# Projections in one block, earlier rotation and casts, and stores of the split parts from ScalarE's queue in a four-layer transformer kernel

## The chip, the cores and the metric

The kernel runs on one core of one Trainium2 chip. The time is the device time of one execution in microseconds (us), lower is better. It is given as the median of three timed runs; one further execution was recorded by the hardware profiler, and all rows of the trace come from that one.

## The reference

The input is x, 2 batches of 1024 tokens with 128 features, float32. Four layers follow one another, each wrapped in layer norms:

```
x = x + layernorm(attention0(layernorm(x)))       # 16 heads of 64, causal
x = x + layernorm(mixture_of_experts(layernorm(x)))  # 8 experts, top 2, 128 -> 256 -> 128, exact GELU
x = x + layernorm(attention1(layernorm(x)))       # 16 heads of 8, rotary embedding
x = x + layernorm(bit_linear_ffn(layernorm(x)))   # ternary weights, relu squared
```

The change touches the seam between the second and the third layer. There it is computed, for each batch of 1024 tokens:

```
QKV = layernorm(x) @ qkv.T
q = Q * cos + rotate_half(Q) * sin                # the same for k
scores = q @ k.T / sqrt(8)                        # per head, causal; a score of exactly 0 is masked
```

## The kernel before

The five engines run programs of their own, written out by hand and tied together by semaphores. Tokens lie in four banks of 512 (NB), two for each batch. One program order per engine is fixed, so a waiting instruction holds everything behind it on its engine.

**The experts.** The mixture of experts is computed densely, one expert after the other: m = 0 to 7 for batch 0 and m = 8 to 15 for batch 1 (E is 8, so m == E + 2 is m = 10). TensorE runs, for each m, up(m + 1) and then down(m) (lines 1333 on). up(m) is four units, each a 128x512 block of hidden values into one of two banks; unit u waits until ScalarE has made the GELU of unit u - 2 (h_ready, line 1298). ScalarE makes gelus(m), four of them. down(m) fills two banks, and VectorE's sums(m) adds each of them to acc as soon as it is complete (4 operations of 128x128). down(m) waits for the sums of the expert before it.

**Attention 1's preparation for batch 0**, which rides along with batch 1's experts:

- Projections: for each of the two banks j, five products project1(j, which, bank): Q, Q with swapped halves, K, K with swapped halves, V. TensorE makes the five of j = 0 behind down(10) and the five of j = 1 behind down(11) (lines 1343 to 1351), and four PSUM banks rotate (PROJ1). ScalarE copies each out (projected1, lines 743 to 748), behind gelus(11) and gelus(12).
- Rotation: for i = 0 (Q) and i = 1 (K), VectorE multiplies the straight half by cos (rotate("cos", i), line 862), GpSimd the swapped half by sin (line 596), and VectorE adds the two (rotate("add", i), line 866). VectorE has cos 0 and cos 1 behind sums(11), add 0 and add 1 behind sums(12).
- Splitting: each float32 value becomes three bfloat16 parts. ScalarE casts the value (part(i, 0), line 639), VectorE subtracts the part (left(i, 0), line 871), ScalarE casts the rest (part(i, 1)), VectorE subtracts again and so writes the third part (left(i, 1)). ScalarE has part(0, 0) and part(1, 0) behind gelus(13), part(0, 1) and part(1, 1) behind gelus(14). VectorE has left(., 0) behind the adds and left(., 1) behind sums(13).
- Stores: SyncE writes the parts to HBM, store(0) and store(1) of 768 KB each (line 473), behind its loads of the experts' weights, the last of which waits for down(13). When both have landed (part_stored), it reads them back as stacks: stacks(half) is 18 DMAs of 64 KB, nine into QS and nine into KS, each into 8 partitions (lines 452 to 467). stacks(0) is issued first, then stacks(1).

**Attention 1** starts on TensorE when the ten copies are done, pO is cleared by VectorE behind the last sums (line 1089), and stacks(0) has landed. Batch 1's own projections, rotation and parts are made during batch 0's attention and stored by store(2) and store(3).

The numbers on a split part: split_step_of(i, j) is the count that part_a (casts) and part_v (differences) have reached when step j of part i is done.

Of the kernel before, what the change touches and what calls it, by code (L numbers as in the profile page):

```python
# [24 lines left out]
B, S, D = 2, 1024, 128  # L25
# [13 lines left out]
E, TOPK, F0 = 8, 2, 256  # L39
# [6 lines left out]
NPROB = 3  # L46
TBANKS = 3
PROJ1 = (6, 7, 2, 3)
QUEUED = 4
NMASK = 3  # L50
EPS = 1e-5
# [138 lines left out]
def build(nc, x, w0, wo0, router_w, router_b, w1, b1, w2, b2, wl1, wo1, fast_bT, w_fc, w_proj, uT, v, gate,  # L190
          consts, rotary, out):
    with ExitStack() as ctx:
# [165 lines left out]
        def split_step_of(i, j):  # L358


            return 2 * j + i + 1 if i < 2 else 2 * i + j + 1
# [4 lines left out]
        def part_of(i):  # L366
            return parts0[:, i, :, :] if i < 2 else parts1[:, :, :]

        def rotated(i, swapped):
            return rot[i // 2][:, 2 * (i % 2) + swapped, :]  # L370

# [4 lines left out]
        def _(sp):  # L376
# [92 lines left out]
            def store(i):  # L469
                sp.wait_ge(part_a, split_step_of(i, 1))  # L470
                sp.wait_ge(part_v, split_step_of(i, 1))
                b = i // 2
                sp.dma_start(split[i % 2, :, :, b * S:(b + 1) * S].rearrange("k p s -> p k s"), part_of(i)).then_inc(part_stored, 16)

            store(0)
            store(1)
            sp.wait_ge(part_stored, 32)
            stacks(0)
            stacks(1)
# [16 lines left out]
        def _(pool):  # L496
# [83 lines left out]
            for b in range(B):  # L580
                banks = range(b * NB // B, (b + 1) * NB // B)
                for j in banks:
                    power_of(2, 0, j)
                for j in banks:
                    pool.wait_ge(yn_ready[2], j + 1)
                    t = slice(j * TPB, (j + 1) * TPB)
                    pool.tensor_tensor(X[:, t, :], X[:, t, :], yn2[:, j % 2, :, :], ALU.add).then_inc(x_added[2], 1)
                for j in banks:
                    power_of(2, 1, j)
                pool.wait_ge(ld_rot, 32)  # L590
                for i in (2 * b, 2 * b + 1):
                    if b == 0:
                        pool.wait_ge(proj1_copied, 5 + 2 * i + 2)
                    else:
                        pool.wait_ge(A[1]["cp_act"], L[1].side_copied("Q", (3, 2 * (i - 2) + 1)))
                    pool.tensor_tensor(rotated(i, 1), rotated(i, 1), sin[:, :], ALU.mult).then_inc(rope_sin, 1)
# [5 lines left out]
        def _(act):  # L602
# [134 lines left out]
            for m in range(1, B * E):  # L737
                gelus(m)
                if m == E + 3:
                    for j in range(2):  # L740
                        act.wait_ge(tr_done[2], j + 1)
                        nc.scalar.copy(xnT[:, j * BANK:(j + 1) * BANK], bank[2 + j]).then_inc(xnT_ready[2], 1)
                if m in (E + 3, E + 4):
                    j = m - E - 3
                    for what in range(5):
                        u = j * 5 + what
                        act.wait_ge(proj1, u + 1)
                        projected1(j, what, bank[PROJ1[u % len(PROJ1)]]).then_inc(proj1_copied, 1)
                if m in (E + 5, E + 6):
                    part(0, m - E - 5)  # L750
                    part(1, m - E - 5)
            attention(1)


# [16 lines left out]
        def _(dve):  # L771
# [83 lines left out]
            def rotate(what, i):  # L855
                if what == "cos":
                    dve.wait_ge(ld_rot, 32)
                    if i < 2:
                        dve.wait_ge(proj1_copied, 5 + 2 * i + 1)
                    else:  # L860
                        dve.wait_ge(A[1]["cp_act"], L[1].side_copied("Q", (3, 2 * (i - 2))))
                    nc.vector.tensor_tensor(rotated(i, 0), rotated(i, 0), cos[:, :], ALU.mult).then_inc(rope_cos, 1)
                else:
                    dve.wait_ge(rope_cos, i + 1)
                    dve.wait_ge(rope_sin, i + 1)
                    nc.vector.tensor_tensor(rotated(i, 0), rotated(i, 0), rotated(i, 1), ALU.add).then_inc(rope_done, 1)
# [206 lines left out]
                    sums(E + "ym yn xm xn".split().index(what) // 2, ("ym yn xm xn".split().index(what) % 2,))  # L1073
            sums(E + 1, (1,))
            sums(E + 2, (0, 1))
            sums(E + 3, (0, 1))
            rotate("cos", 0)
            rotate("cos", 1)
            sums(E + 4, (0, 1))
            rotate("add", 0)  # L1080
            rotate("add", 1)
            left(0, 0)
            left(1, 0)
            sums(E + 5, (0, 1))
            left(0, 1)
            left(1, 1)
            sums(E + 6, (0, 1))
            sums(E + 7, (0, 1))
            nc.vector.memset(pO[:, 0:P], 0.0).then_inc(pO_cleared, 1)
# [6 lines left out]
        def _(pe):  # L1096
# [238 lines left out]
            for m in range(B * E):  # L1335
# [4 lines left out]
                    for j in range(2):  # L1340
                        transpose1(j, bank[2 + j]).then_inc(tr_done[2], 1)
                down(m)
                if m in (E + 2, E + 3):
                    j = m - E - 2
                    pe.wait_ge(xnT_ready[2], 2)
                    pe.wait_ge(added, NT + E * ST)
                    for which in range(5):
                        u = j * 5 + which
                        if u >= len(PROJ1):
                            pe.wait_ge(proj1_copied, u - len(PROJ1) + 1)  # L1350
                        project1(j, which, bank[PROJ1[u % len(PROJ1)]]).then_inc(proj1, 1)
# [70 lines left out]
```

## Time and profile before

| | us |
|---|---|
| timed runs | 1264.19, 1263.3, 1258.38 |
| median | 1263.3 |
| profiled execution | 1254.74 |
| its span, first to last instruction | 1252.9 |
| TensorE matmul busy | 1112.5 |
| VectorE busy | 862.9 |
| ScalarE busy | 814.4 |
| GpSimd busy | 349.4 |

The span is what the trace covers; the 1.8 us beside it lie before the first and behind the last instruction. The experts of batch 1 run from about 677 to 753 us of the span, attention 1 from 769 us on. In the views PE is TensorE, DVE VectorE, ACT ScalarE, POOL GpSimd, SP SyncE, and SPq what SyncE's queue issues. L and a number is a line of the kernel. A time in a timeline is the start in us from the span's start, followed by the duration; a group of several instructions stands as one row with its count, and the brackets at the end hold the idle time of the engine ahead of it and what ended it.

### The profile page before, as it was taken

The page shows a single profiled execution, that of the slowest core. Times are in us where ns is not written, and L with a number is a line of the kernel's source. Part 1 is how long each engine was busy: PE and PEld are TensorE (multiplying, and loading weights), DVE is VectorE, ACT ScalarE, POOL GpSimd, SP SyncE. Part 2 cuts the span into 40 slices and gives each one's busy share as a digit, 9 for nine tenths or more (in the row PEclk, how much of TensorE's full clock was granted, in tenths as well). Part 3 has the DMA queues.
Part 4 walks back from the last instruction along what each step waited for, and adds up shares of the span by engine and source line. Part 5 has one row for each costly group of instructions (what it writes and reads, how often), then busy time and mean ns, then how long its engine had stood idle before and what let it go on. Part 6 is the DMA issues. An engine that isn't in the chain of part 4 may idle for free.

```text
span 1252.9 us, 28180 instructions
## 1 busy us (share of the span) xinstructions
PE 1112.5 (89%) x10202; PEld 844.8 (67%) x10202; DVE 862.9 (69%) x2486; ACT 814.4 (65%) x1915; POOL 349.4 (28%) x345
## 2 busy tenths in 40 slices
PE   3799999999999999999799983897788888888886
PEld 1587878787888878789566661565556556556674
DVE  4565656565656565655433554999999999999954
ACT  2566666666666676750234441898989989989923
POOL 1596464545455555504000111010000000000033
PEclk9899999999999999999699995898999999999999
DMA  3222232222223232200101115020302212110001
GB/s 109 70 57 68 59 85 59 71 73 69 75 68 75 68 76 69 68 19 26 39 26 43 30 69 74 3 39 27 64 8 33 27 14 40 18 24 2 2 1 34
DMA packets 33147, 58.90 MB, mean 47 GB/s; under 512 B 4810, under 2 KB 18018, under 8 KB 33010
## 3 DMA queue, kind: packets, MB, share of 16 engines
q1 hardware_dynamic: 33010, 57.10, 20.0%
q8 instruction: 83, 1.36, 0.5%
q14 instruction: 54, 0.44, 0.1%
HBM read 27.59 MB, written 4.33 MB: 25 GB/s over the span
## 4 chain that ended last, share of the span: by engine, by line
PE 56%; DVE 18%; issue 11%; ACT 7%; POOL 5%; DMA 3%; SPq 1%; ACTq 0%; POOLq 0%; DVEq 0%
PE pT L1237 12%; PE pO L1160 12%; PE pS L1198 10%; DVE Zb L914 9%; PE pS L1299 4%; PE pT L1108 4%; PE pT L1312 3%; ACT probs L688 3%; DVE Sm L929 3%; PE pS L1260 2%; PE pT L1112 2%; ACT PT L668 1%; PE pS L1379 1%; PE pS L1359 1%; DMA KS<-split 1%
## 5 line engine op out<-in xcount | busy, mean ns | idle before, releaser
L1237 PE MATMUL pT<-cst,probs 128*128 128x128 f32 x2304 | 367.1, 285 | 55.2 <-ACT probs L688 50.9
L1237 PEld LDWEIGHTS pT<-cst,probs 128*128 128x128 f32 x2304 | 255.2, 142 | 149.5 <-ACT probs L688 100.3
L688 ACT ACTIVATE probs<-probs,nmax 128x128 f32<-128x128 f32 (+7 forms) x256 | 198.6, 776 | 131.9 <-DVE nmax L924 130.9
L668 ACT COPY PT<-pT 128x512 f32<-128x512 f32 (+3 forms) x576 | 263.1, 480 | 15.0 <-PE pT L1237 13.9
L924 DVE CUSTOM_DVE_ANT_0 probs<-pS,causal_wide 128x128 f32<-128x128 f32 (+7 forms) x256 | 192.0, 750 | 92.9 <-PE pS L1198 85.2
L688 ACT ACTIVATE probs<-Sm,nmax 128x128 f32<-128x128 f32 (+7 forms) x256 | 199.4, 779 | 61.2 <-DVE nmax L929 55.4
L1160 PE MATMUL pO<-PT,V 128*64 128x128 f32 (+1 forms) x4608 | 231.4, 279 | 1.9 <-DVE attnT L883 1.1
L914 DVE TENSOR_SCALAR Zb<-pS 128x128 bf16<-128x128 f32 (+7 forms) x256 | 192.7, 753 | 21.5 <-PE pS L1204 21.2
L1160 PEld LDWEIGHTS pO<-PT,V 128*64 128x64 f32 (+1 forms) x4608 | 180.6, 114 | 34.4 <-issue 19.9
L929 DVE CUSTOM_DVE_ANT_0 Sm<-pS,Zb 128x128 f32<-128x128 f32 (+7 forms) x256 | 193.3, 755 | 4.5
L512 POOL TENSOR_TENSOR rstd<-rstd,power 128x4 f32<-128x4 f32 x32 | 32.6, 1017 | 553.3 <-DVE rstd L782 553.2
L966 DVE COPY PT<-pT 128x256 f32<-128x256 f32 (+3 forms) x192 | 99.8, 520 | 115.9 <-PE pT L1237 114.6
L1198 PE MATMUL pS<-Kh,Qs 128*128 128x512 f32 (+2 forms) x384 | 159.0, 423 | 7.2 <-DMA Kl<-Kl 7.2
L1198 PE MATMUL pS<-KS,QS 72*128 72x512 bf16 (+3 forms) x384 | 108.4, 337 | 25.8 <-DMA KS<-split 15.9
L1198 PE MATMUL pS<-Kl,Qs 128*128 128x512 f32 (+2 forms) x384 | 128.8, 344 | 0.0
L1198 PEld LDWEIGHTS pS<-Kh,Qs 128*128 128x128 f32 x384 | 73.3, 191 | 27.8 <-issue 21.6
L1198 PEld LDWEIGHTS pS<-Kl,Qs 128*128 128x128 f32 x384 | 73.5, 191 | 20.3 <-issue 14.6
L729 ACT ACTIVATE hT<-pS,b1s 128x512 f32<-128x512 f32 x64 | 43.7, 687 | 57.2 <-PE pS L1299 57.2
L555 POOL TENSOR_TENSOR Ql<-raw,Qs 64x512 fp32r<-64x512 f32 x60 | 76.5, 1276 | 4.8
L555 POOL TENSOR_TENSOR Kl<-raw,Kh 64x512 fp32r<-64x512 f32 x60 | 76.5, 1275 | 4.8
L1064 DVE SCALAR_TENSOR_TENSOR acc<-pT,router,acc 128x128 f32<-128x128 f32 x112 | 31.5, 344 | 66.1 <-PE pT L1312 66.1
L575 POOL TENSOR_TENSOR attnT<-attnT,wq_t 128x1024 f32<-128x1024 f32 x16 | 38.3, 2391 | 118.9 <-DMA wq_t<-factors 118.4
(183 smaller groups left out, 1361.5 us busy)
## 6 DMA issues: line engine op xcount, KB each, us to landing
Qs<-Ql SPq DMA_DIRECT2D x32, 256.0 KB, 3.7
Kh<-Kh SPq DMA_DIRECT2D x32, 256.0 KB, 3.4
Kl<-Kl SPq DMA_DIRECT2D x32, 256.0 KB, 4.6
wq_t<-factors SPq DMA_DIRECT2D x32, 256.0 KB, 4.0
QS<-split SPq DMA_DIRECT2D x72, 64.0 KB
KS<-split SPq DMA_DIRECT2D x72, 64.0 KB
split<-parts SPq DMA_DIRECT2D x4, 768.0 KB, 4.0
w1s<-in_w SPq DMA_DIRECT2D x16, 128.0 KB, 2.2
```

The costliest lines, as they stand in the source:

```text
L555: i = pool.tensor_tensor(low[h], source[rows[h], :], high[h].bitcast(F32), ALU.subtract)
L668: nc.scalar.copy(PT[:, g % 2, h, k0 * P:(k0 + nk) * P], pT[r % TBANKS][:, 0:nk * P])\
L688: nc.scalar.activation(probs[:, i % NPROB, 0:n], src[:, 0:n], ACT.Exp, bias=nmax[:, i % 4:i % 4 + 1], scale=-1.0, accum_out=total).then_in ...
L914: nc.vector.tensor_scalar(Zb[:, i % NMASK, 0:n], pS[i % 2][:, 0:n], 0.0, MASKED, ALU.is_equal, ALU.mult).then_inc(a["z"], 1)
L924: nc.vector.tensor_tensor_reduce(probs[:, i % NPROB, 0:n], pS[i % 2][:, shift(k, qt):shift(k, qt) + n], causal_wide[:, S - n:S], -1.0, 3e3 ...
L929: nc.vector.tensor_tensor_reduce(Sm[:, i % NMASK, 0:n], pS[i % 2][:, 0:n], Zb[:, i % NMASK, 0:n], -(DH1 ** -0.5), 3e38, ALU.add, ALU.min, ...
L966: nc.vector.tensor_copy(PT[:, gg % 2, hh, k0 * P:(k0 + nk) * P], pT[r % TBANKS][:, 0:nk * P])\
L1108: return nc.tensor.matmul(p, w0s[:, what, :], xnT[:, b * S + j * BANK:b * S + (j + 1) * BANK], start=True, stop=True)
L1160: m = nc.tensor.matmul(pO[rows, 0:P], v, PT[:, g % 2, h, kt * P:(kt + 1) * P], start=(kt == 0), stop=(kt == qt), skip_group_check=True)
L1198: m = nc.tensor.matmul(pS[i % 2][:, (off + c0) * P:(off + c1) * P], lhs, keys[:, b if k == 0 else half % 2, h, c0 * P:c1 * P], start=(n == 0),
L1237: m = nc.tensor.transpose(pT[r % TBANKS][:, kt * P:(kt + 1) * P], probs[:, item % NPROB, (k0 + kt) * P:(k0 + kt + 1) * P], ident)
L1299: nc.tensor.matmul(bank[u % 4 if m < E else u % 2], w1s[:, m % 2, f * P:(f + 1) * P], xnT[:, j * BANK:(j + 1) * BANK], start=True, stop=Tr ...
```

## The change

Six edits, in the order of the data:

1. TensorE makes all ten projections behind down(10). Their order is now by kind, both banks of each kind after one another (PROJECTIONS), so that Q is complete with the second, its swapped form with the fourth, K with the sixth and its swapped form with the eighth.
2. ScalarE copies all ten behind gelus(11).
3. The waits for proj1_copied follow: 4i + 2 for cos (before 5 + 2i + 1), 4i + 4 for sin (before 5 + 2i + 2).
4. VectorE has cos 0, cos 1 and add 0 ahead of sums(11), add 1 and left(., 0) behind it, left(., 1) behind sums(12), and sums(13) after that.
5. ScalarE has part(., 0) behind gelus(12) and part(., 1) behind gelus(13).
6. store(0) and store(1) are issued by ScalarE behind gelus(14), after it has waited for both kinds of split step. SyncE only waits for part_stored. store(2) and store(3) stay on SyncE.

```diff
+PROJECTIONS = [(j, which) for which in (0, 1, 2, 3, 4) for j in range(2)]
...
+        def split_of(i):
+            return split[i % 2, :, :, i // 2 * S:(i // 2 + 1) * S].rearrange("k p s -> p k s")
...
             def store(i):
                 sp.wait_ge(part_a, split_step_of(i, 1))
                 sp.wait_ge(part_v, split_step_of(i, 1))
-                b = i // 2
-                sp.dma_start(split[i % 2, :, :, b * S:(b + 1) * S].rearrange("k p s -> p k s"), part_of(i)).then_inc(part_stored, 16)
-
-            store(0)
-            store(1)
+                sp.dma_start(split_of(i), part_of(i)).then_inc(part_stored, 16)
+
             sp.wait_ge(part_stored, 32)
             stacks(0)
...
                     if b == 0:
-                        pool.wait_ge(proj1_copied, 5 + 2 * i + 2)
+                        pool.wait_ge(proj1_copied, 4 * i + 4)
...
-                if m in (E + 3, E + 4):
-                    j = m - E - 3
-                    for what in range(5):
-                        u = j * 5 + what
+                if m == E + 3:
+                    for u, (j, what) in enumerate(PROJECTIONS):
                         act.wait_ge(proj1, u + 1)
                         projected1(j, what, bank[PROJ1[u % len(PROJ1)]]).then_inc(proj1_copied, 1)
-                if m in (E + 5, E + 6):
-                    part(0, m - E - 5)
-                    part(1, m - E - 5)
+                if m in (E + 4, E + 5):
+                    part(0, m - E - 4)
+                    part(1, m - E - 4)
+                if m == E + 6:
+                    for i in range(2):
+                        act.wait_ge(part_a, split_step_of(i, 1))
+                        act.wait_ge(part_v, split_step_of(i, 1))
+                        nc.scalar.dma_start(split_of(i), part_of(i)).then_inc(part_stored, 16)
...
                     if i < 2:
-                        dve.wait_ge(proj1_copied, 5 + 2 * i + 1)
+                        dve.wait_ge(proj1_copied, 4 * i + 2)
...
             sums(E + 2, (0, 1))
-            sums(E + 3, (0, 1))
             rotate("cos", 0)
             rotate("cos", 1)
-            sums(E + 4, (0, 1))
             rotate("add", 0)
+            sums(E + 3, (0, 1))
             rotate("add", 1)
             left(0, 0)
             left(1, 0)
-            sums(E + 5, (0, 1))
+            sums(E + 4, (0, 1))
             left(0, 1)
             left(1, 1)
+            sums(E + 5, (0, 1))
             sums(E + 6, (0, 1))
...
-                if m in (E + 2, E + 3):
-                    j = m - E - 2
+                if m == E + 2:
                     pe.wait_ge(xnT_ready[2], 2)
                     pe.wait_ge(added, NT + E * ST)
-                    for which in range(5):
-                        u = j * 5 + which
+                    for u, (j, which) in enumerate(PROJECTIONS):
```

## Rows read from the trace of the kernel before

**Rows 1.** The page's first section: busy us of each engine, share of the span, instructions.
```profile
PE 1112.5 (89%) x10202; PEld 844.8 (67%) x10202; DVE 862.9 (69%) x2486; ACT 814.4 (65%) x1915; POOL 349.4 (28%) x345
```

**Rows 2.** Waits, 670 to 770 us: who waited for whom, us, times, longest.
```profile
PE pS L1198 <- DMA KS<-split: 15.9, 1, 15.9
```

**Rows 3.** The chain that ended last, 730 to 880 us: start, us, what.
```profile
746.06 4.43 DMA split<-parts
756.35 12.78 DMA KS<-split
```

**Rows 4.** Timeline of TensorE, 675 to 770 us: start, duration, operation, count.
```profile
706.95 1.02 PE L1124 MATMUL pT<-xnT,wl1s 128*128 128x512 f32 x2
...
711.27 3.79 PE L1299 MATMUL pS<-xnT,w1s 128*128 128x512 f32 x8
714.90 3.73 PE L1312 MATMUL pT<-w2s,hT 128*128 128x128 f32 x32
...
722.79 3.79 PE L1299 MATMUL pS<-xnT,w1s 128*128 128x512 f32 x8
...
735.30 3.65 PE L1299 MATMUL pS<-xnT,w1s 128*128 128x512 f32 x4 [3.43 <-ACT hT L729]
738.74 3.81 PE L1312 MATMUL pT<-w2s,hT 128*128 128x128 f32 x32
...
746.01 7.31 PE L1312 MATMUL pT<-w2s,hT 128*128 128x128 f32 x64
769.26 0.27 PE L1198 MATMUL pS<-KS,QS 72*128 72x128 bf16 x1 [15.94 <-DMA KS<-split]
```

**Rows 5.** Timeline of VectorE, 675 to 770 us.
```profile
716.88 1.13 DVE L1064 SCALAR_TENSOR_TENSOR acc<-pT,router,acc 128x128 f32<-128x128 f32 x4 [8.61 <-PE pT L1312]
...
720.22 1.22 DVE L862 TENSOR_TENSOR rot<-rot,cos 128x1024 f32<-128x1024 f32 x1 [0.42 <-ACT rot L630]
721.93 2.80 DVE L862 TENSOR_TENSOR rot<-rot,cos 128x1024 f32<-128x1024 f32 x1 [0.49 <-ACT rot L630]
...
743.64 2.35 DVE L871 TENSOR_TENSOR parts<-rot,parts 128x1024 bf16<-128x1024 f32 x2
...
754.51 0.17 DVE L1089 MEMSET pO<- 128x128 f32 x1
```

**Rows 6.** Timeline of SyncE's queue, 670 to 770 us: issues.
```profile
742.59 0.38 SPq L450 DMA_DIRECT2D w2s<-in_w  x1
744.93 1.50 SPq L473 DMA_DIRECT2D split<-parts  x2
750.50 0.30 SPq L464 DMA_DIRECT2D QS<-split  x1
...
756.35 0.30 SPq L466 DMA_DIRECT2D KS<-split  x1
```

**Rows 7.** Windows: stretch, us, engines' busy us (x instructions), PEclk (1.00 is full), DMA share, GB/s.
```profile
735.30:737.00 1.70, 1.70 (x2) 0.71 (x3) 0.62 (x1) 0.53 (x1) 0.00 (x0) 0.55 0.00 0
745.00:750.00 5.00, 5.00 (x39) 4.47 (x39) 2.32 (x6) 2.66 (x3) 0.00 (x0) 1.00 0.84 314
753.00:769.00 16.00, 0.32 (x3) 0.13 (x2) 1.29 (x5) 0.00 (x0) 0.00 (x0) 0.59 0.55 72
```

**Rows 8.** Timeline of ScalarE, 675 to 770 us.
```profile
708.01 0.58 ACT L630 COPY rot<-pT 128x512 f32<-128x512 f32 x1 [3.66 <-PE pT L1124]
708.87 0.58 ACT L630 COPY rot<-pO 128x512 f32<-128x512 f32 x1 [0.27 <-PE pO L1124]
...
726.62 0.69 ACT L729 ACTIVATE hT<-pS,b1s 128x512 f32<-128x512 f32 x1 [0.17 <-PE pS L1299]
```

**Rows 9.** Timeline of GpSimd, 675 to 770 us.
```profile
721.11 5.82 POOL L596 TENSOR_TENSOR rot<-rot,sin 128x1024 f32<-128x1024 f32 x2 [21.98 <-ACT rot L630]
```

**Rows 10.** The parts' tile: the stores (count, min/median/max ns of an issue) and their landing.
```profile
L473 SPq DMA_DIRECT2D split<-parts x4: 366/380/382, 744.9 to 885.0; - x4
...
DMA to landing us min/median/max: 3.5/4.0/5.3
```

## The prediction

> **What bounds the kernel now.** I read the page first: TensorE has by far the largest busy share, 89% [rows 1], so a gain must shorten a stretch in which it runs or waits. The waits of the stretch from batch 1's experts to the second attention come next. Two waits of TensorE stand out there: 15.9 us of the first score matmul for the stacked K parts (KS) [rows 2], and 3.43 us of an expert's first-layer matmul (L1299) for a GELU [rows 4]. The chain in order of time says what the large one is made of: the stores of the split parts (4.43 us to landing), then 18 stack loads, of which the last takes 12.78 us to land [rows 3]. The timelines give the dates. TensorE ends the last expert at 746.01 + 7.31 = 753.32 and starts attention at 769.26 [rows 4]. VectorE clears pO by 754.51 + 0.17 = 754.68 [rows 5]. SyncE issues the stores at 744.93, goes on at 750.50 with the stacks and issues the last one of stacks(0) at 756.35 [rows 6]. So attention starts when the parts have gone out and come back, 14.6 us after everything else is ready. Whatever moves the landing of stacks(0) moves attention, and what follows it, until that slack is gone.
>
> How long is the round trip? From the first store's issue to the first stack's: 750.50 - 744.93 = 5.57 us. From there to attention: 769.26 - 750.50 = 18.76 us. The stacks are limited by the transfer: in 753 to 769 us the queues move 72 GB/s at a DMA share of 0.55, while the stores moved 314 GB/s [rows 7]. An earlier start doesn't change either speed, so I take both durations over unchanged.
>
> **1. The projections in one block.** Five take 711.27 - 706.95 = 4.32 us of TensorE [rows 4]; the other five move ahead of up(12) and down(11) and cost the same 4.32. The copies on ScalarE follow one every 0.86 us (708.01, 708.87) and take 0.58 [rows 8]; four banks rotate, and the copy four back is long done, so TensorE doesn't wait. Ten projections last 706.95 to 715.59, then up(12) 3.63, down(11) 3.57: up(13) starts at 722.79 as before. On TensorE this part alone is worth nothing. What it buys is the dates of the copies: the second (Q complete) ends at 708.87 + 0.58 = 709.45 instead of 720.11, the fourth at 711.2, the sixth at 712.9, the eighth at 714.6.
>
> **2. Rotation earlier.** VectorE is free between sums(10), over by the time of the first copy, and down(11)'s first half. That half comes 1.98 us after down's start in today's rows (716.88 against 714.90) [rows 4, 5], so at 719.22 + 1.98 = 721.2. In between go cos 0 (1.22 us, from 709.6) and cos 1 (from 713.0), and GpSimd's two sine products (5.82 us for both now [rows 9]) from 711.3 to at most 719. cos 1 takes 2.80 us today beside GpSimd, against 1.22 alone [rows 5]; priced at 2.80 it ends at 715.8, and "add 0" at 2.8 more ends by 718.6. All of it fits ahead of 721.2, so it costs nothing; if it didn't, sums(11) would slip by the rest, and TensorE needs those sums only at down(12), 7 us later. Then sums(11) ends near 724.0 and "add 1" (half of 2.35) at 725.2.
>
> **3. Casts earlier.** ScalarE ends gelu(12) at 715.59 + 4.52 = 720.1 (4.52 is from up's start 722.79 to gelu's end 726.62 + 0.69 [rows 4, 8]). It casts part(0,0), then waits for "add 1" until 725.2 and casts until 726.25. Behind this wait stand the GELUs of expert 13, and behind them TensorE: up(13) can do two of its four units (722.79 to 724.67) and then waits for gelu(13) unit 0, some 0.65 us long. It goes on at 726.9, a wait of 2.3 us. So the 3.4 us wait isn't removed; it moves one expert ahead and shrinks by 1.1 to 1.2 us.
>
> **4. The clock behind that wait.** Today the last two units after the wait (735.30 to 738.74) take 3.44 us instead of 1.81, and the granted clock there is 0.55 of full, that is the lower level of 1.2 GHz [rows 4, 7]; the loss is 1.63 us. Before it TensorE stood still for 3.43 us. After a wait of 2.3 us the clock may hold or fall: 0 or 1.63 us. I take 0, since the wait is a third shorter and TensorE is busy throughout before it, and keep 1.63 for the range.
>
> **5. To the end of gelu(14).** The rest of up(13) ends at 726.9 + 1.81 = 728.7, down(12) at 732.3, gelu(14) at 732.3 + 4.52 = 736.8. Meanwhile ScalarE makes the second casts after gelu(13) (729.5 to 731.6, ahead of the first unit of up(14) at 733.4, so hidden), and VectorE does sums(12) until 733.6 and then the two last differences (2.35 us [rows 5]) until 736.0, 0.8 us ahead of 736.8. Should they be late, ScalarE waits in front of gelu(15), whose first unit arrives only at 739.5 + 1.06 = 740.5 (1.06 from the start of a product of this shape, 706.95, to its reader, 708.01 [rows 4, 8]): 3.7 us of cover.
>
> **6. Stores from ScalarE's queue.** On SyncE they would stand behind the load of w2s for expert 15, which waits for down(13): 742.59 today [rows 6], 739.5 then. From ScalarE they go at 736.9. No row shows a DMA issued by ScalarE. On SyncE an issue holds the queue 0.38 us; even ten times that would be covered by the 3.7 us ahead of gelu(15). The landing I bound by rows: 5.57 us from first issue now, of which the second store, issued last, needs 4.43 [rows 3, 6]. With both issued together it lies between 4.43 + 0.38 = 4.8 and, by the longest landing of a store (5.3) behind the 1.50 that the two issues take today, 6.8 [rows 6, 10]. I take 5.57, as both are held up by 1.57 MB going through. Landed: 742.5. The Trainium skill speaks against this part ("DMA: Bandwidth & Descriptors", "Issuing engines are not separate DMA queues"): starting DMAs on several engines only saves the sequencer's issue time. By that alone the two issues, 0.76 us, would be all; [rows 6] show a wait for down(13) ahead of them in the same queue, and that, 2.6 us, is what I count.
>
> **7. The stacks.** SyncE waits there by 739.9 and issues stacks(0) at 742.5; they land at 742.5 + 18.76 = 761.3. Next latest are TensorE at 753.32 - 2.8 = 750.5 and the clearing of pO at 751.9, so the stacks still decide, with some 10 us to spare. The sum: 769.26 - 761.3 = 8.0 us. Attention then starts after an idle of over 10 us, as today after 15.9 us, and the clock has every reason to be where it is today (0.59 over 753 to 769 [rows 7]), so nothing is added or lost behind it; batch 1's own parts stay with SyncE.
>
> **The sum and the time.** The profiled execution lasted 1254.74 us, its span 1252.9; minus 8.0 that is 1246.7. The median of the three timed runs is 1263.3, 8.6 above the profiled one, and I forecast against it: 1263.3 - 8.0 = 1255.3 us.
>
> **The rivals.**
> (a) The clock falls behind the new wait too. All from up(13) to gelu(14) then moves 1.63 us back, since ScalarE can issue the stores only behind gelu(14): gain 6.4 us, 1256.9. For it: the same shape of wait dropped it today. Against it: 2.3 us is shorter. Chance 0.2.
> (b) ScalarE's queue is dearer than SyncE's, or casts and sums slip past gelu(14): 2 to 5 us of the gain go. The margin of VectorE in step 5 is only 0.8 us. Near 1259. Chance 0.17.
> (c) The order doesn't bring what it says: the wait for "add 1" grows (sine products and sums in one another's way), TensorE stands as long as now, and the stores get away little earlier than now. About 1262. Chance 0.08.
> (d) Slower: the stores from ScalarE run at the stacks' speed instead of the stores' own. 1.57 MB at 72 GB/s [rows 7] is 21.8 us instead of 5.6; they would land at 736.9 + 21.8 = 758.7 and attention would start at 777.5, 8.2 us later than now: 1271.5. It decides from a landing of 5.6 + 8.0 = 13.6 us. The four stores of today, of the same shape, all landed within 3.5 to 5.3 us [rows 10], which speaks against it. Chance 0.05.
>
> **How the numbers follow.** The likeliest case, steps 1 to 7 with gains of 7 to 9 us, has 0.5. The range takes in (a), (b) and most of (c), and the spread of the runs shown (1258.38 to 1264.19): 1247.5 to 1263. Half a percent is 6.3 us, about what a measurement of this kernel can tell from no change. The likeliest case lies 1.7 us past it, (a) at its edge, (b) and (c) within: faster 0.57, within 0.37, slower 0.06.
>
> **What would show it.** In the changed profile: ten L1124/L1126 projections in a row from about 707 to 715.6; TensorE's wait for hT near 724.7 of about 2.3 us, with a granted clock of 1.0 behind it (0.55 is (a)); stores issued on ScalarE's queue near 737, some 8 us ahead of today's; the first stack 5.6 us behind them; attention near 761.3, with a wait of TensorE for KS of 10.8 us instead of 15.9; the distance from there to the end as now, some 484 us. The prediction is wrong if the first stack comes more than 7 us after the stores' issue, if gelu(14) ends after 738.5, or if the stacks take clearly more or less than 18.8 us.

## The result and the profile after

| | before | after |
|---|---|---|
| median of 12 timed runs, us | 1263.59 | 1252.61 |
| lowest to highest, us | 1258.29 to 1266.76 | 1249.19 to 1257.91 |
| span of the profiled execution, us | 1252.9 | 1250.1 |

The ratio of after to before is 0.9932, with a 95% interval of 0.9913 to 0.9951. Two later batches gave 0.9962 (0.9943 to 0.9981) and 0.9938 (0.9915 to 0.9961) for the same kernel. So the change makes the kernel faster, by 0.4 to 0.7%, that is 5 to 9 us, with 7 us as the mean of the three ratios. The forecast was 8.0 us. The two medians of a batch lie 11.0, 7.0 and 8.1 us apart. In the first batch the runs of the kernel before fall into two groups, four at 1258.3 to 1259.1 and eight at 1263.3 to 1266.8, and a median taken from such groups jumps, so the text goes by the ratios.

The two spans differ by only 2.8 us. That is the first thing to explain, because the prediction was worked out on the profiled execution.

TensorE in the changed kernel (timeline: start, duration, operation, count, idle time ahead of it and what ended it), to be held against [rows 4]:

```profile
707.04 1.02 PE L1128 MATMUL pT<-xnT,wl1s 128*128 128x512 f32 x2
...
715.69 3.79 PE L1303 MATMUL pS<-xnT,w1s 128*128 128x512 f32 x8
...
722.89 1.88 PE L1303 MATMUL pS<-xnT,w1s 128*128 128x512 f32 x4
727.07 1.98 PE L1303 MATMUL pS<-xnT,w1s 128*128 128x512 f32 x4 [2.30 <-ACT hT L730]
728.89 3.73 PE L1316 MATMUL pT<-w2s,hT 128*128 128x128 f32 x32
...
743.27 7.31 PE L1316 MATMUL pT<-w2s,hT 128*128 128x128 f32 x64
764.00 0.27 PE L1202 MATMUL pS<-KS,QS 72*128 72x128 bf16 x1 [13.42 <-DMA KS<-split]
```

The ten projections fill 707.04 to 715.69. The wait for a GELU is there, one expert earlier, and lasts 2.30 us instead of 3.43. Attention starts at 764.00 instead of 769.26.

VectorE, for [rows 5], and GpSimd, for [rows 9]:

```profile
713.08 1.76 DVE L866 TENSOR_TENSOR rot<-rot,cos 128x1024 f32<-128x1024 f32 x1 [2.21 <-ACT rot L631]
714.76 1.21 DVE L870 TENSOR_TENSOR rot<-rot 128x1024 f32<-128x1024 f32 x1
...
724.13 1.22 DVE L870 TENSOR_TENSOR rot<-rot 128x1024 f32<-128x1024 f32 x1
...
733.70 2.35 DVE L875 TENSOR_TENSOR parts<-rot,parts 128x1024 bf16<-128x1024 f32 x2
```

```profile
711.40 2.35 POOL L597 TENSOR_TENSOR rot<-rot,sin 128x1024 f32<-128x1024 f32 x1 [12.18 <-ACT rot L631]
714.77 3.41 POOL L597 TENSOR_TENSOR rot<-rot,sin 128x1024 f32<-128x1024 f32 x1 [1.02 <-ACT rot L631]
```

The second add starts only at 724.13, behind sums(11), though its two inputs were ready at 718.2. ScalarE, for [rows 8], with the stores that are now in its stream (ACTq):

```profile
720.10 1.03 ACT L640 CAST parts<-rot 128x1024 bf16<-128x1024 f32 x1
725.38 1.04 ACT L640 CAST parts<-rot 128x1024 bf16<-128x1024 f32 x1 [4.24 <-DVE rot L870]
...
736.28 0.69 ACT L730 ACTIVATE hT<-pS,b1s 128x512 f32<-128x512 f32 x1 [0.17 <-PE pS L1303]
736.34 2.51 ACTq L755 DMA_DIRECT2D split<-parts  x2
740.71 0.69 ACT L730 ACTIVATE hT<-pS,b1s 128x512 f32<-128x512 f32 x1 [3.74 <-PE pS L1303]
```

SyncE's queue, for [rows 6]:

```profile
739.85 0.38 SPq L454 DMA_DIRECT2D w2s<-in_w  x1
743.00 0.30 SPq L468 DMA_DIRECT2D QS<-split  x1
```

And two windows, for [rows 7]: behind the wait the clock is at its upper level (1.00, 2.4 GHz); the stacks' transfer moves 63 GB/s where the kernel before had 72.

```profile
727.07:728.90 1.83, 1.83 (x5) 0.87 (x6) 0.61 (x1) 1.19 (x2) 0.00 (x0) 1.00 0.00 0
743.00:764.00 21.00, 7.58 (x66) 7.18 (x65) 4.67 (x17) 2.27 (x3) 0.00 (x0) 0.73 0.52 63
```

Where the 8 us went in this pair of executions can be added up. The first stack is 7.5 us earlier (743.00 against 750.50). The transfer of stacks(0) takes 21.0 us instead of 18.76, which gives 2.24 back. Attention to the third layer's output projection takes 423.2 us (764.00 to 1187.16) instead of 422.3 (769.26 to 1191.59), which costs 0.83. The rest takes 62.9 us instead of 61.3, which costs 1.63 more, and this last part is one row: the last product of the kernel ran 5.47 us in the changed kernel and 3.84 us in the one before. First the row of the kernel before, then that of the changed one:

```profile
1240.84 3.84 PE L1379 MATMUL pS<-wq_t,relu 128*128 128x128 f32 x32 [1.92 <-ACT relu L767]
```

```profile
1236.41 5.47 PE L1381 MATMUL pS<-wq_t,relu 128*128 128x128 f32 x32 [1.92 <-ACT relu L771]
```

7.5 - 2.24 - 0.83 - 1.63 = 2.8 us. The question for the experiments is which of these belong to the change and which to the execution.

### The profile page after: what moved, and what is told of

The parts are those of the page before. It is cut to its first block, busy times and chain, and to the rows that moved or that the text cites. A ratio compares the mean times of both kernels' runs of the same rounds, so it can differ in the third digit from the quotient of the medians.

```text
span 1250.1 us, 28179 instructions
## 1 busy us (share of the span) xinstructions
PE 1113.9 (89%) x10202; PEld 846.4 (68%) x10202; DVE 862.7 (69%) x2486; ACT 814.1 (65%) x1915; POOL 349.3 (28%) x345
## 4 chain that ended last, share of the span: by engine, by line
PE 55%; DVE 18%; issue 11%; ACT 6%; POOL 5%; DMA 3%; SPq 1%; ACTq 0%; POOLq 0%; DVEq 0%
PE pT L1241 12%; PE pO L1164 12%; PE pS L1202 10%; DVE Zb L918 9%; PE pS L1303 4%; PE pT L1112 4%; DVE Sm L933 3%; PE pT L1316 3%; ACT probs L689 3%; PE pS L1264 2%; PE pT L1116 2%; PE pS L1381 1%; DMA KS<-split 1%; PE pS L1361 1%; ACT PT L669 1%
```

## The experiments

Theory: attention starts when stacks(0) has landed; the change moves the first stack by some 7.5 to 8 us and nothing else. Rivals: the change also slows the stacks, as they now start while the experts still run; an issue on another queue is worth only its own time; the wait for a GELU isn't on the path; something other than the stacks' landing sets the start.

To compare executions, all dates in the table are counted from the first projection (the first L1124 or L1128 row of TensorE's timeline), since that date itself moves from execution to execution (last column). First store and first stack are the issues of these DMAs, attention is the first score product, and transfer is the time from the first stack's issue to it. Each row is one profiled execution.

| kernel | first store | first stack | experts end | attention | transfer | first projection |
|---|---|---|---|---|---|---|
| before | 37.98 | 43.6 | 46.4 | 62.3 | 18.8 | 706.95 |
| again_before | 37.95 | 43.5 | 46.3 | 64.3 | 20.8 | 711.67 |
| block_only | 37.97 | 43.5 | 46.4 | 64.5 | 21.0 | 711.14 |
| after | 29.30 | 36.0 | 43.5 | 57.0 | 21.0 | 707.04 |
| again_after | 29.30 | 36.0 | 43.5 | 57.1 | 21.1 | 705.83 |
| again_after2 | 29.30 | 35.2 | 43.5 | 54.0 | 18.7 | 706.75 |
| stores_sync | 33.3 | 39.0 | 43.6 | 59.9 | 20.9 | 707.01 |
| add_first | 26.9 | 32.8 | 41.2 | 54.0 | 21.2 | 711.60 |
| store_twice | 35.5 (second pair) | 41.1 | 46.4 | 61.9 | 20.8 | 705.62 |
| stacks1_late | 29.30 | 36.0 | 43.5 | 55.0 | 19.0 | 711.09 |
| order_fast | 24.2 | 31.6 | 41.2 | 52.5 | 21.0 | 708.69 |
| fast_late | 24.2 | 31.6 | 41.2 | 52.0 | 20.4 | 711.86 |
| keys_gpsimd | 29.30 | 35.7 | 43.5 | 54.4 | 18.7 | 711.64 |
| fast_late_gpsimd | 24.2 | 31.2 | 41.2 | 47.1 | 15.9 | 708.13 |

The time in us behind each name below is the median of its 4 to 12 timed runs; the ratio is to the kernel before in the same batch, with its 95% interval.

**The two kernels again.** No edit.

> The kernel before once more, unaltered, for its profile. Its profiled execution lasted 1254.74 us, below each of its 59 timed ones, and its stacks(0) took 18.76 us to land, while seven others with the same loads took 20.8 to 21.2. If that 18.76 was a favourable execution, this one shows about 21.0 us from the first stack to attention and 1257 to 1265 us in all; if the kernel before has the shorter transfer as its own (its stacks begin when the experts are nearly over), it shows 18.8 again. Counted from its first projection, the stores are issued at 37.98 and the first stack at 43.56 in either case.

> The changed kernel once more, unaltered. In its profile the dates up to the first stack load came out as forecast (stores issued at 736.3, first stack at 743.0), but stacks(0) took 21.0 us to land instead of the 18.76 us of before, and from the start of attention to the end it took 486.1 us instead of 483.6. If both are chance of the one execution, this profile shows again 743.0 for the first stack (within 0.3), a transfer that may as well be 18.8 us, and another distance to the end. If the change slows the stacks (their first loads now run beside the last experts), the transfer is 21 us again. Timed: 0.993 of before, by the theory that the date of the first stack moves everything by some 7.5 us.

> The changed kernel a third time, on the chip of the three others of this batch. Dates counted from the first projection: stores at 29.3, first stack at 36.0, attention at 57.0 (transfer 21). Time between 0.993 and 0.996 of before, between the two ratios measured so far.

Measured: again_before 1261.5 us, again_after 1256.2 us with 0.9962, again_after2 1253.4 us with 0.9938. The profile of again_before, TensorE and the window of the transfer:

```profile
711.67 1.02 PE L1124 MATMUL pT<-xnT,wl1s 128*128 128x512 f32 x2
...
775.93 0.26 PE L1198 MATMUL pS<-KS,QS 72*128 72x128 bf16 x1 [17.92 <-DMA KS<-split]
```

```profile
755.18:775.90 20.72, 2.82 (x26) 2.64 (x25) 2.83 (x11) 0.00 (x0) 0.00 (x0) 0.66 0.52 64
```

The same of again_after2:

```profile
706.75 1.02 PE L1128 MATMUL pT<-xnT,wl1s 128*128 128x512 f32 x2
...
760.70 0.27 PE L1202 MATMUL pS<-KS,QS 72*128 72x128 bf16 x1 [10.40 <-DMA KS<-split]
```

```profile
742.00:760.70 18.70, 8.29 (x67) 7.63 (x67) 4.67 (x17) 2.66 (x3) 0.00 (x0) 0.78 0.52 72
```

Both kernels show both transfers: 18.7 or 18.8 us at 72 GB/s and about 21 us at 63 to 64 GB/s. The change isn't what slows the stacks: again_before has the slower transfer without it and again_after2 the faster one with it. The profiled execution of before was one with the faster transfer. Like with like, the gain at the start of attention is 64.3 - 57.0 = 7.3 us with the slower transfer and 62.3 - 54.0 = 8.3 us with the faster one. Of the 1.0 us between these two, 0.7 lies in the landing of the stores, as the first stack of again_after2 comes at 35.2 instead of 36.0. The slower transfer doesn't use fewer DMA engines: the share is 0.52 in both, and the packets moved are nearly as many (814 in before, 804 in the changed kernel), so a packet takes some 14% longer. Why stays open.

The last column explains a part of the rest of the scatter. Up to the first projection the programs are the same, and still that date lies between 705.6 and 711.9. The windows of 600 to 640 us, where the router ends and the first experts start, show why. Before, then again_before, and below each of them its row of the same 24 products:

```profile
600.00:640.00 40.00, 34.45 (x153) 24.04 (x153) 14.42 (x90) 12.61 (x19) 0.00 (x0) 0.76 0.12 37
622.66 3.01 PE L1331 MATMUL pT<-b2s,wgT 8*128 8x128 f32 x24
```

```profile
600.00:640.00 40.00, 35.49 (x136) 25.16 (x135) 13.30 (x86) 9.86 (x15) 0.00 (x0) 0.60 0.09 30
623.26 5.48 PE L1331 MATMUL pT<-b2s,wgT 8*128 8x128 f32 x24
```

A granted clock of 0.76 against 0.60 (a mean of its two levels), and 153 against 136 products done. The first projection comes 4.7 us later, of which 0.6 is there ahead of these 24 products: more than half of what the change is worth, between two executions of one kernel. All fourteen profiles go this way: the six with the first projection at 711.1 to 711.9 have a granted clock of 0.60 or 0.61 in this stretch, the eight at 705.6 to 708.7 have 0.72 to 0.79.

Two more parts scatter behind the start of attention. From there to the kernel's last product it takes 471.6 to 476.1 us, which no experiment here explains, and that product itself takes 3.84 us in two profiles (before, fast_late) and 5.46 or 5.47 in the other twelve, the one of again_before among them. So the profile that the prediction was worked out on had the faster transfer, the shortest attention and the faster last product.

**block_only**: the first part alone.

```diff
-                if m in (E + 2, E + 3):
-                    j = m - E - 2
+                if m == E + 2:
...
-                    for which in range(5):
-                        u = j * 5 + which
+                    for u, (j, which) in enumerate(PROJECTIONS):
...
-                        pool.wait_ge(proj1_copied, 5 + 2 * i + 2)
+                        pool.wait_ge(proj1_copied, 4 * i + 4)
...
-                        dve.wait_ge(proj1_copied, 5 + 2 * i + 1)
+                        dve.wait_ge(proj1_copied, 4 * i + 2)
```

(ScalarE's copies likewise.)

> The kernel before with the first part of the change alone: ten projections in one block, ScalarE's ten copies behind gelus(11), the waits for the copies renumbered; rotation, casts and stores stay where they are. Theory: the block alone is worth nothing, because the casts still come behind sums(12) and gelus(13). TensorE's wait for a GELU shrinks only if the adds do come earlier, which they can't, as they stand behind sums(12). VectorE's cos 1 no longer meets GpSimd, but nobody waits for it. First stack at 750.5, attention near 769.3, time as before, within 0.2%. Rival (the earlier copies pay by themselves): part of the 8 us shows.

Measured: 1260.2 us, ratio 0.9984 (0.9958 to 1.001).

```profile
711.14 1.02 PE L1123 MATMUL pT<-xnT,wl1s 128*128 128x512 f32 x2
...
739.51 3.02 PE L1298 MATMUL pS<-xnT,w1s 128*128 128x512 f32 x4 [3.44 <-ACT hT L730]
```

From the first projection on, every date is that of before within 0.1 us, the 3.44 us wait included. The block is worth nothing by itself on the path. The median is 2.9 us below that of before in its batch and its interval takes in 1, so it doesn't contradict that.

**stores_sync**: part 6 undone.

```diff
-                if m == E + 6:
-                    for i in range(2):
-                        act.wait_ge(part_a, split_step_of(i, 1))
-                        act.wait_ge(part_v, split_step_of(i, 1))
-                        nc.scalar.dma_start(split_of(i), part_of(i)).then_inc(part_stored, 16)
...
+            store(0)
+            store(1)
             sp.wait_ge(part_stored, 32)
```

> The changed kernel with the two stores back on SyncE's queue, behind the load of w2s for expert 15. Theory (head of the line): the stores are issued at 740.3, when that load has been issued (739.85 + 0.4), instead of 736.3 on ScalarE; the first stack follows 5.6 us later, at 745.9 instead of 743.0, and attention starts 2.9 us later than in the changed kernel; time 1255.5. Rival (an issue on another queue only saves the time of issuing): start within 0.8 us of the changed kernel's, time unchanged at 1252.6.

Measured: 1259.2 us, ratio 0.9979 (0.9959 to 1.0); again_after in the same batch had 0.9962.

```profile
739.82 0.38 SPq L454 DMA_DIRECT2D w2s<-in_w  x1
740.30 0.94 SPq L476 DMA_DIRECT2D split<-parts  x2
745.99 0.30 SPq L468 DMA_DIRECT2D QS<-split  x1
```

The stores stand right behind the load that waits for down(13), as expected to the tenth, 4.0 us later than in the changed kernel; they land in 5.7 us instead of 6.7, and so attention is 3.0 us later (59.92 against 56.96). The medians differ by 3.0 us too, though the two intervals overlap, so the dates carry this reading. (The 1255.5 us expected had been counted from 1252.6 for the changed kernel, and that had 1256.2 in this batch.) ScalarE's queue saves a place in line. The rest of the gain, 64.3 or 64.5 (again_before, block_only) to 59.9, is 4.3 to 4.6 us and belongs to the earlier rotation and casts, which need the block. The Trainium skill ("DMA: Bandwidth & Descriptors", "Issuing engines are not separate DMA queues") counts only the sequencer's issue time; the trace shows 0.94 us for both issues, and attention 3.0 us earlier, because the queue passed by was waiting.

**add_first**: the second add ahead of sums(11).

```diff
             rotate("add", 0)
-            sums(E + 3, (0, 1))
             rotate("add", 1)
+            sums(E + 3, (0, 1))
```

> The changed kernel with VectorE's second add ahead of sums(11) instead of behind it. Both sine products are over at 718.2, the sums come at 721.3, so the add (1.2 us) fits. ScalarE's second cast then follows the first at once (721.1 to 722.2), gelus(13) isn't held up, and TensorE's wait of 2.30 us disappears. Theory (the chain of forecast steps 3 to 7): everything behind up(13) comes 2.3 us earlier, stores at 734.0, first stack at 740.7, attention 2.3 us earlier than in the changed kernel; time 1250.3. Rival (the wait isn't on the path, as attention waits for the stacks and TensorE has slack): TensorE's experts end 2.3 us earlier, but attention starts at the same time.

Measured: 1250.7 us, ratio 0.9916 (0.9887 to 0.9944), 5.4 us under again_after in its batch. TensorE has no wait for a GELU any more; up(13) runs through in one piece, and the stores follow:

```profile
727.45 3.79 PE L1303 MATMUL pS<-xnT,w1s 128*128 128x512 f32 x8
```

```profile
738.53 1.50 ACTq L755 DMA_DIRECT2D split<-parts  x2
```

Counted from the first projection, the stores come at 26.9 instead of 29.3, which is the 2.3 us of the wait, and attention at 54.0 instead of 57.0 with the same slower transfer. So the wait was on the path, by way of gelus(14) and not by way of the experts. The other 0.7 us is the landing of the stores, 5.9 us instead of 6.7, below. The 5.4 us between the medians is more than the 3.0 us that the dates show; the two intervals leave room for that.

**store_twice**: the outward trip doubled (the declarations of spare and spared are left out).

```diff
+                        nc.scalar.dma_start(spare[i, :, :, 0:S].rearrange("k p s -> p k s"), part_of(i)).then_inc(spared, 16)
+                    act.wait_ge(spared, 32)
+                    for i in range(2):
                         nc.scalar.dma_start(split_of(i), part_of(i)).then_inc(part_stored, 16)
```

> The changed kernel in which ScalarE first stores both parts (1.57 MB) to a spare place in HBM, waits until they have landed and then stores them again to their own place. It doubles the outward half of the round trip. Theory: the first stack comes some 6.5 us later (from 743.0 to 749.5), and attention with it, from near 763 to 769.5; gelus(15) are held up by the wait too, up to 742.9, some 2 us, which has no price since TensorE's experts still end by 753.5. Time 1259 to 1260. Rival (attention is set by something else, such as the experts): well under 6 us.

Measured: 1260.0 us, ratio 0.9994 (0.9975 to 1.0013).

```profile
734.92 2.02 ACTq L757 DMA_DIRECT2D spare<-parts  x2
741.15 0.91 ACTq L760 DMA_DIRECT2D split<-parts  x2
742.10 1.26 ACT L732 ACTIVATE hT<-pS,b1s 128x512 f32<-128x512 f32 x2 [6.56 <-DMA spare<-parts]
```

The first stack comes 5.1 us later than in the changed kernel, not 6.5, since the second pair landed 5.6 us after its issue, and attention comes 5.0 us later, with a transfer of 20.8 us. Of the 7.3 us that the change gains with the slower transfer 2.4 are left (64.3 against 61.9); the ratio of 0.9994 is back near 1, and its interval leaves room for such a rest. The experts end at 46.4, 15.6 us ahead of attention, so they don't set its start; the landing of the parts does.

**stacks1_late** and **fast_late**: stacks(1) only after four score tiles.

```diff
             stacks(0)
+            sp.wait_ge(A[1]["s"], 4)
             stacks(1)
```

> The changed kernel in which SyncE issues stacks(1) only after the first four score tiles, so that stacks(0) has the queues for itself. Theory (the loads of one queue go one after the other on each DMA engine, and the engines that a stack uses are full from stacks(0) alone): its transfer takes 18.8 to 21 us as before, at most 1 us less. Rival (stacks(1) takes a share): by the 0.15 MB that it moved in that time next to the 1.18 MB of stacks(0), 2 to 2.5 us less, with attention earlier by as much.

> The faster order (second add ahead of sums(11), differences between the halves of the sums, stores between the GELUs of expert 14) and stacks(1) issued only after four score tiles. Counted from the first projection the first stack comes at 31.6, as in the faster order alone. Theory (stacks(1) takes a share of the DMA engines, 0.14 MB of 1.32 in the transfer): the transfer is 19.0 us instead of 21.0, as it was with stacks(1) held back in the changed kernel, attention at 50.5 instead of 52.5, time 0.988 of before. Rival (the 18.97 us was a favourable execution like the one of before): 21 us, time 0.989.

Measured: stacks1_late 1253.6 us, 0.9933 (0.9904 to 0.9962), transfer 19.0 us; fast_late, on top of order_fast below, 1251.0 us, 0.9917 (0.9899 to 0.9936), transfer 20.4 us. The first seemed to bear out that stacks(1) takes a share. The second, by its own expectation, speaks for the rival: 20.4 us instead of the 19.0 hoped for, and no gain over order_fast. Between these two, holding stacks(1) back saves 0.6 us of the 21. The 19.0 us is near the 18.7 that the kernels unaltered in this respect show too, though here 1.18 MB was moved in it instead of some 1.35; what part of it was the hold can't be told from one profile.

**order_fast**: everything as early as the experts' order allows (store(i) has the two waits and the issue; the block behind gelus(14) goes).

```diff
             rotate("add", 0)
-            sums(E + 3, (0, 1))
             rotate("add", 1)
+            sums(E + 3, (0,))
             left(0, 0)
+            sums(E + 3, (1,))
             left(1, 0)
-            sums(E + 4, (0, 1))
+            sums(E + 4, (0,))
             left(0, 1)
             left(1, 1)
+            sums(E + 4, (1,))
...
+                    if m == E + 6 and u in (1, 3):
+                        store(u // 2)
```

> The changed kernel, built so that the parts are finished as early as this order of the experts allows: second add ahead of sums(11), each difference between the two halves of sums(11) and sums(12), and the stores issued by ScalarE between the GELUs of expert 14 (the first ahead of unit 1, the second ahead of unit 3). Expected dates: no wait of TensorE at up(13), last difference done near 732, stores at 731.5 and 734, landed near 738, first stack 5 us earlier than in the changed kernel (738 against 743.0), attention 5 us earlier. Stores of 1.25 us each hold up the GELUs of expert 14, and TensorE with them by 1 to 2 us, without a price, as TensorE has 13 us of slack. Time 1247.5. Rival (holding up the GELUs costs the clock or the path): above 1250.

Measured: 1249.7 us, ratio 0.9891 (0.9869 to 0.9913).

```profile
732.79 0.69 ACT L737 ACTIVATE hT<-pS,b1s 128x512 f32<-128x512 f32 x1 [1.87 <-PE pS L1307]
732.85 0.38 ACTq L728 DMA_DIRECT2D split<-parts  x1
733.65 0.69 ACT L737 ACTIVATE hT<-pS,b1s 128x512 f32<-128x512 f32 x1 [0.17 <-PE pS L1307]
734.69 0.69 ACT L737 ACTIVATE hT<-pS,b1s 128x512 f32<-128x512 f32 x1 [0.36 <-PE pS L1307]
734.75 0.37 ACTq L728 DMA_DIRECT2D split<-parts  x1
```

Attention comes 4.4 us earlier than in the changed kernel, with the same transfer of 21.0 us. The GELUs are not held up at all, where over 1 us for each store was expected: each issue takes 0.37 us and runs beside the GELU ahead of it.

**keys_gpsimd** and **fast_late_gpsimd**: the nine K loads of stacks(0) from GpSimd's queue; the second on top of fast_late.

```diff
+                if b == 0:
+                    pool.wait_ge(part_stored, 32)
+                    for row in range(0, STACK, DH1):
+                        j = row // DH1 % PARTS
+                        pool.dma_start(KS[row:row + DH1, 0, :, :],
+                                       split[1, j:j + 1, 0:HPG * DH1, 0:S].rearrange("k (h d) s -> k d h s", h=HPG)
+                                       .rearrange("k d h s -> (k d) h s")).then_inc(ld_keys, 16)
```

(SyncE leaves them out, and TensorE waits for ld_keys too.)

> The changed kernel in which the nine K loads of stacks(0) are issued by GpSimd, while SyncE issues the nine Q loads and then stacks(1). In the trace the loads of 8 partitions use the DMA queues at a share of 0.55 and 63 to 72 GB/s, whereas the stores of 128 partitions went at 314. Theory (the stacks' own transfer, 18.8 to 21 us, is the largest term, and it is slow because each load runs on half of the DMA engines): if GpSimd's loads go to other engines too, the transfer falls to 12 to 15 us, attention starts 5 to 8 us earlier than in the changed kernel, time 1245 to 1248. The Trainium skill ("DMA: Bandwidth & Descriptors", "Why a DMA increments its semaphore by 16 and not by 1") says that GpSimd's loads take their engines in turn and SyncE's always the lowest-numbered ones. Rival (all loads go to the same engines): nothing, or a loss by GpSimd's slower issue.

> The same, and the nine K loads of stacks(0) issued by GpSimd. With stacks(1) behind SyncE's nine Q loads, GpSimd's loads landed 5.9 us after their issue (median) and the last one 13.6 us, while the DMA share rose from 0.55 to 0.87 for a while. Theory (GpSimd's loads use the DMA engines that SyncE's leave idle, and only those that meet SyncE's are slow): with stacks(1) held back SyncE's queue is empty after some 0.59 MB, 9 to 10 us, so the transfer falls to 10 to 13 us and attention starts at 42 to 45, close behind the end of the experts at 41.2. Time 0.982 to 0.985 of before, 1241 to 1245. Rival (something else makes the loads slow, such as the distance to HBM): 17 to 19 us, no faster than the version without GpSimd.

Measured: keys_gpsimd 1253.9 us, 0.9919 (0.9898 to 0.9941), transfer 18.7 us; fast_late_gpsimd 1242.7 us, **0.9851 (0.9832 to 0.9871)**, transfer 15.9 us. In keys_gpsimd the transfer was no shorter than the faster level of the other kernels, a miss: the last K load landed 13.6 us after its issue, beside the loads of stacks(1). With stacks(1) held back the last one takes 10.8 us. The windows of fast_late_gpsimd, and the landing of GpSimd's loads:

```profile
739.36:744.50 5.14, 5.14 (x30) 3.35 (x29) 0.86 (x4) 4.03 (x5) 4.86 (x9) 1.00 0.72 128
744.50:750.00 5.50, 4.80 (x43) 4.61 (x42) 3.52 (x14) 0.00 (x0) 0.23 (x1) 1.00 0.67 73
750.00:755.20 5.20, 0.00 (x0) 0.00 (x0) 0.63 (x3) 0.00 (x0) 0.00 (x0) 0.67 0.38 49
```

```profile
DMA to landing us min/median/max: 4.6/5.4/10.8
```

The DMA share is 0.72 and 0.67, against 0.53 and 0.56 in the same two stretches of fast_late, and falls to 0.38 at the end: more DMA engines work at first, and then some of them have nothing left. The transfer was neither the 10 to 13 us of the theory nor the 17 to 19 of the rival. The direction agrees with what the Trainium skill says ("DMA: Bandwidth & Descriptors", "Why a DMA increments its semaphore by 16 and not by 1"): by its rule a load of 8 partitions runs on 8 engines, from SyncE always on the 8 lowest-numbered ones, from GpSimd on 8 consecutive ones that move on in turn. The trace here names no single DMA engine, so the size of the effect is shown and its mechanism isn't. This version beats both kernels: 1242.7 us, 18.7 us below the 1261.4 of before in its batch, and 10.6 below again_after2. Against fast_late attention starts 4.9 us earlier while the medians are 8.3 us apart; by the two intervals 5 to 12 us are possible, and no row accounts for more than the 4.9.

## Why the prediction was right, point by point

**What bounds the kernel**: right. The start of attention followed the first stack in all kernels, by a transfer of 18.7 to 21.2 us as long as SyncE alone loads, whatever was done to the experts; block_only and store_twice bracket it.

**Steps 1 to 3** (block, rotation, casts): right to 0.1 us, counted from the first projection. up(13) starts at 722.89 (forecast 722.79, and the first projection was itself 0.09 later), the second cast at 725.38, TensorE's wait is 2.30 us (2.3). cos 1 took 1.76 us where 2.80 was allowed for; nobody waited for it.

**Step 4** (the clock): right. The two units behind the wait take 728.89 - 727.07 = 1.82 us at a granted clock of 1.00. In all seven profiles with a wait of 2.3 us at up(13) they did; with 3.43 to 3.44 us, in the three profiles of the old order, the clock fell, to 0.55, 0.83 and 0.72 over the same 1.82 us. It cost the same each time: from the end of the wait to the start of up(15) it took 7.0 or 7.1 us, where the same work takes 5.4 in the changed kernel (727.07 to 732.46). A wait of 2.73 us ahead of up(15)'s third unit in store_twice left the clock at 1.00 too. Rival (a) is out here.

**Steps 5 and 6**: the date of the stores was forecast 0.6 us too late and their landing 0.4 to 1.2 us too short, so the two nearly cancel. ScalarE issues the first store at 736.34, while its last GELU runs from 736.28 to 736.97; the sum had waited for the GELU's end. From first store to first stack it took 6.7 us in after, again_after and stacks1_late, 6.4 in keys_gpsimd, and 5.9 in again_after2 and add_first, where 5.57 was taken and 4.8 to 6.8 allowed. The row of the issues shows where it lies: the pair takes 2.51 us of ScalarE, of which the second issue, 0.48 us behind the first, takes 2.0, while two issues 1.9 us apart take 0.37 each (order_fast) and SyncE's pair 0.94 (stores_sync). It isn't ScalarE's queue alone that makes it: ScalarE's second pair in store_twice took 0.91 and landed in 5.6 us. What does stays open. It was covered as forecast: gelus(15) start at 740.71, 1.9 us after the pair ends.

**Step 7** (the stacks): the term that was mis-sized, and by the prediction's own sign ("clearly more or less than 18.8 us") a miss in the profile after: 21.0 us. 18.76 us was taken over unchanged from one execution. It is one of two levels: of the nine other profiles with the loads issued as in the kernel before, eight show 20.8 to 21.2 us and one 18.7. As both kernels have both levels, this shifts the profiled spans and hardly the difference: 7.3 us at one level, 8.3 at the other, 8.0 forecast. The profile after alone shows only 5.3 us (769.26 to 764.00), and from there to the end 486.1 us where 484 was expected.

**The sum against the median**: the forecast of 1255.3 us lay 2.7 us above the 1252.6 measured. The gain on the path was right, with some luck: the stores were forecast too late and their landing too short, two errors that nearly cancelled, and the transfer's error falls on both kernels. The scatter of the executions decides the rest: the same kernel later had 1256.2 and 1253.4. The prediction named the spread of the runs but not its source; the profiles show four parts of it, the clock between 600 and 640 us, the transfer, attention, and 1.6 us at the very end. Rival (b) came in part, as 0.4 to 1.2 us of landing, and not as the 2 to 5 us that it was given; (c) would have shown as a longer wait, (d) as a landing over 13.6 us, and neither did.

## What to carry to other kernels

When a stage starts on a round trip through HBM, count the trip from its first issue back through what stands in program order ahead of it: here a cast behind an add behind another expert's sums, and a store behind a load that waited for a matmul. These two were worth 2.3 us (add_first) and 3.0 us (stores_sync), and none of it was work. Compare executions by dates counted from an event that the programs share, and take a duration on which the sum rests from more than one execution. What was left once the order was right, 21 us of loads at a DMA share of about a half, is where the next gain was.

## What the runs showed of the hardware

- The same 18 loads land in 18.7 or in 21 us, while the queues move 72 or 63 GB/s at the same DMA share of 0.52. Why is open.
- ScalarE issues a DMA while the activation ahead of it still runs (736.34 against an end of 736.97). A second store of 768 KB issued 0.5 us behind the first held it 1.0 us (add_first, 1.50 for the pair) to 2.1 us (again_after, 2.61), but only 0.5 us in the second pair of store_twice (0.91); 1.9 us behind, 0.37 us.
- GpSimd's nine loads of 64 KB, beside SyncE's, landed in 5.4 us (median), and raised the DMA share from 0.53 (fast_late) to 0.72 in the first 5.1 us.
- Two executions of one kernel differed by 4.7 us at the first projection, at a granted clock of 0.76 against 0.60 over the 40 us from 600 on.
- Behind a wait of TensorE of 2.3 us (seven profiles) the granted clock was 1.00, behind one of 3.4 us (three profiles) 0.55 to 0.83 over the next 1.82 us.
